# The last step of a block inverse: the inverse added by VectorE at the eviction instead of by identity products on TensorE

## The reference, cut to what matters

```python
S = S * exp(g_t)
mem = einsum('bhk,bhkv->bhv', k_t, S)
delta = (v_t - mem) * b_t
S = S + einsum('bhk,bhv->bhkv', k_t, delta)
o_t = einsum('bhk,bhkv->bhv', q_t * scale, S)
```

## Time and profile before

| | before |
|---|---|
| median of 3 executions | 4767.14 us (4764.29 to 4769.24) |
| span of the profiled execution | 4761.7 us |
| TensorE matmul busy | 4665.0 us (98%) |
| VectorE busy | 4138.2 us (87%) |
| ScalarE busy | 3397.1 us (71%) |
| GpSimd busy | 3152.1 us (66%) |

### The profile page before, as it was taken

How to read it: one execution, slowest core, us unless ns; L and a number is a source line. 1 busy time by engine, 2 the same in 40 slices (tenths; PEclk the granted TensorE clock), 3 DMA queues, 4 the chain that set the end, 5 groups by cost and what they waited for, 6 DMA issues and landing times. The chain is left out here.

```text
span 4761.7 us, 140986 instructions
## 1 busy us (share of the span) xinstructions
PE 4665.0 (98%) x44336; PEld 3733.8 (78%) x44336; DVE 4138.2 (87%) x9914; ACT 3397.1 (71%) x10287; POOL 3152.1 (66%) x4511
## 2 busy tenths in 40 slices
PE   6999999999999999999999999999999999999798
PEld 4788888888888888888888888888888888888566
DVE  6888888888888888888888888888888889999576
ACT  5777777777777777777777777777777777777443
POOL 5666666666666666666666666666666666777565
PEclk9999999999999999999999999999999999999899
DMA  5111111111111111111111111111111111121000
GB/s 180 48 33 44 33 53 34 44 37 47 46 34 44 33 53 33 44 33 51 36 44 35 42 50 36 44 34 50 35 44 33 44 42 53 47 61 44 29 29 34
DMA packets 206732, 212.94 MB, mean 45 GB/s; under 512 B 17218, under 2 KB 180180, under 8 KB 206036
## 3 DMA queue, kind: packets, MB, share of 16 engines
q1 hardware_dynamic: 206036, 204.06, 14.0%
HBM read 186.31 MB, written 17.70 MB: 43 GB/s over the span
## 5 line engine op out<-in xcount | busy, mean ns | idle before, releaser
L1074 DVE SCALAR_TENSOR_TENSOR cv<-ps_a,wqkv,cv 128x511 f32<-128x511 f32 (+2 forms) x1536 | 1145.8, 746 | 181.6 <-ACT cv L1067 161.0
L1279 POOL TENSOR_TENSOR bm<-bat,mask 128x256 f16<-128x256 f32 x1536 | 1029.5, 691 | 0.6
L1059 PE MATMUL ps_a<-xin,wqkv 128*128 128x512 f32 x2048 | 1002.8, 612 | 3.0 <-DVE bat L1256 1.5
L1329 ACT ACTIVATE m<-b 128x256 f16<-128x256 f32 x1536 | 597.2, 389 | 376.2 <-PE b L1324 376.2
L1067 ACT ACTIVATE cv<-ps_a,wqkv 128x512 f32<-128x512 f32 x512 | 352.0, 688 | 554.3 <-PE ps_a L1059 554.1
L1340 DVE TENSOR_TENSOR tt<-tt,b 128x256 f16<-128x256 f16 x1536 | 635.4, 414 | 115.4 <-PE b L1335 114.8
L1382 ACT CAST tt<-bu 128x256 f16<-128x256 f32 x1536 | 578.2, 376 | 1.2 <-PE bu L1377 0.5
L1514 PE MATMUL ps_a<-wout,yT 128*128 128x256 f32 x2048 | 548.3, 390 | 0.5 <-ACT yT L1508 0.5
L1059 PEld LDWEIGHTS ps_a<-xin,wqkv 128*128 128x128 f32 x2048 | 349.6, 191 | 250.6 <-issue 250.6
L1207 PE MATMUL ps_b<-wgate,xin 128*128 128x256 f32 x2048 | 494.9, 384 | 0.2 <-DVE vtok L1230 0.2
L1256 DVE SCALAR_TENSOR_TENSOR bat<-ps_a,w,dec 128x256 f32<-128x256 f32 x1024 | 435.4, 477 | 40.5 <-DVE w L1126 22.4
(11 more groups left out here) (270 smaller groups left out, 12229.8 us busy)
## 6 DMA issues: line engine op xcount, KB each, us to landing
xin<-xT_scratch SPq DMA_DIRECT2D x128, 512.0 KB, 4.0
grow<-g_scratch SPq DMA_DIRECT2D x256, 256.0 KB, 4.6
gam<-g_scratch SPq DMA_DIRECT2D x256, 96.0 KB, 2.8
n_x<-in_x SPq DMA_DIRECT2D x16, 512.0 KB, 4.9
xT_scratch<-acc SPq DMA_DIRECT2D x16, 512.0 KB, 5.9
out_y<-e_yo SPq DMA_DIRECT2D x16, 512.0 KB, 2.6
gate_tok<-in_x SPq DMA_DIRECT2D x56, 128.0 KB, 2.9
wqkv<-in_w_qkv SPq DMA_DIRECT2D x32, 128.0 KB, 3.1
```

The source lines that it names most:

```text
L1059: ins = pe.matmul(ps[:], wqkv[:, k, j * P:(j + 1) * P], xin[p][:, k, :], start=k == 0, stop=k == KT - 1)
L1074: s.done(dve.scalar_tensor_tensor(y[:, r:], ps[:, 0:T - r], tap[:, j, TAPS - 1 - r:TAPS - r], y[:, r:], ALU.mult, ALU.add), f"a_tap{j}{r}")
L1279: s.done(pool.tensor_tensor(half_of(bm[:, l, units(g), :], l, 1), half_of(bt[:, units(g), :], l, 1), half_of(c["mask"][:, l, :].unsqueeze( ...
L1329: s.done(act.mul(half_of(m1[:, l, units(g), :], l, 0), half_bank(bank, l), -1.0), f"b_Me{l}{g}")
```

## The change

`b_F{g}` loses the four products with the identity. `b_T{g}` moves from ScalarE to VectorE and becomes an addition of the bank and `tt[:, 1]`. `b_t2{g}` of the next item, on GpSimd, now waits for `b_T{g}` instead of `b_F{g}`, because `tt[:, 1]` is read by it. In the written order two entries are placed anew: `b_T0.2` stands ahead of `a_tap22.1`, and `b_T1.2` behind `c_R1.2`; the order of all other steps stays.

```diff
-    c_yT2.3 x_y0.5 x_y1.5 b_diag0.1 b_vT0.2 b_t20.1 c_acc1.3 a_tap22.1 c_R3.3 y_sh.0 b_Me31.2 b_T0.2 a_tap23.1
+    c_yT2.3 x_y0.5 x_y1.5 b_diag0.1 b_vT0.2 b_t20.1 c_acc1.3 b_T0.2 a_tap22.1 c_R3.3 y_sh.0 b_Me31.2 a_tap23.1
...
-    c_KS1.2 c_acc3.3 c_p0.2 b_vT1.1 b_E0 b_V20.1 a_tap02 b_U20.1 b_F1.2 b_T1.2 c_R1.2 a_proj1 k_turn.0 c_Z1.2 b_t21.1
+    c_KS1.2 c_acc3.3 c_p0.2 b_vT1.1 b_E0 b_V20.1 a_tap02 b_U20.1 b_F1.2 c_R1.2 b_T1.2 a_proj1 k_turn.0 c_Z1.2 b_t21.1
...
                 if (yield f"b_t2{g}"):
                     s.need(pool, i, f"b_diag{g}")
-                    s.need(pool, i - 1, f"b_F{g}")
+                    s.need(pool, i - 1, f"b_T{g}")
...
                     for k in range(4):
                         u = 4 * g + k
-                        pe.matmul(bank[:, k * P:(k + 1) * P], r16[:, u, :], tt[:, 1, u, :], start=True, stop=False)
-                        ins = pe.matmul(bank[:, k * P:(k + 1) * P], tt[:, 0, u, :], c["ident16"][:], start=False,
-                                        stop=True)
+                        ins = pe.matmul(bank[:, k * P:(k + 1) * P], r16[:, u, :], tt[:, 1, u, :], start=True, stop=True)
                     s.done(ins, f"b_F{g}")
                 if (yield f"b_T{g}"):
-                    s.need(act, i, f"b_F{g}")
-                    s.need(act, i - 2, f"c_Z{2 * g + 1}")
-                    s.done(act.copy(tinv[p][:, units(g), :], in_units(bank)), f"b_T{g}")
+                    s.need(dve, i, f"b_F{g}")
+                    s.need(dve, i - 2, f"c_Z{2 * g + 1}")
+                    s.done(dve.tensor_tensor(tinv[p][:, units(g), :], in_units(bank), tt[:, 1, units(g), :], ALU.add),
+                           f"b_T{g}")
```

## The result

The changed kernel takes 4792.08 us (median of 4 runs, 4791.67 to 4799.81) beside 4765.72 us for the kernel before in the same session (4763.52 to 4769.24, 4 runs): a ratio of 1.0057, 95% interval 1.0046 to 1.0069. It is 26 us slower; the forecast was 20 us slower, in a range that holds 4792.

What follows compares the result with a forecast made beforehand. TensorE was taken as never without work in the attention, with VectorE's chain to the gate close behind. 125 slots x (0.14 - 0.01) = 16 us plus 4 us for late slots, over 4767.1, gave 4787 us, range 4760 to 4812 us.

Steps and rivals of the forecast that it cites:

- The bound: In the attention: TensorE is never without work, but the next chain, on VectorE, may be close behind.
- The removal: In b_F: dropping the identity products frees 0.45 us of TensorE a slot; ScalarE's relief counts as nothing.
- The addition: New b_T on VectorE, once a group: costs 0.60 us to the next start, bounds 0.41 and 0.68 us.
- The gate: Product b_g waits for b_vtok: at least 2.57 us from b_vtok's start to the step behind the gate.
- The sum: Whole kernel: 125 slots give 16 us, late slots 4 us, so 20 us over 4767.1, 4787 us.
- The two groups: In each slot: slack 0.61 us in group 0, 0.46 us in group 1; changes of -0.01 and +0.14 us.
- The late slots: 14 slots with residual steps: c_R2 delays c_Z2, about 0.3 us a slot more, 4 us in all.
- Does the delay end there?: Behind the gates: VectorE's idle times of 0.51 and 0.31 us and smaller waits absorb the delay; nothing further in ordinary slots.
- Rival 3: Behind the gates VectorE does not catch up: 47 us more, 4834 us; chance 0.09.
- GpSimd: b_t2 now waits for b_T: b_t20 follows 0.64 us later, and b_Tq0 does not wait for it.
- Rival 1: TensorE keeps what it was relieved of: slots shorten by 0.45 us, 4709 us; chance 0.12.
- Rival 2: Both sizes nearly cancel, chains 0.05 to 0.1 us shorter: within 0.2%, about 4767 us; chance 0.17.

Runs made afterwards that it cites:

- e1: Kernel before without its identity products; b_T stays a copy on ScalarE, no addition: 4717.23 us, ratio 0.9896.
- e2: Changed kernel with the four identity products put back into b_F, so VectorE's addition is all that is new: 4834.42 us, ratio 1.0141.
- e7: Change made in group 0 alone; group 1 keeps identity products, ScalarE's copy and the old place of b_T1: 4768.17 us, ratio 0.9999.
- e3: Changed kernel with a second, needless addition of half the size behind each b_T on VectorE: 4879.34 us, ratio 1.0236.
- e4: Changed kernel with the addition over two of a group's four units only: 4730.35 us, ratio 0.9919.
- e10: Changed kernel reordered: b_vtok ahead of a conv tap in both groups, a_tanh2 behind c_u3, a_silu2 behind a_tap33, b_hi1 behind b_Ue20: 4788.85 us, ratio 1.0043.
- e12: As e10, but b_Ve31 ahead of b_vtok0 and a_tap23 on VectorE, and b_Ve30 ahead of the statistics: 4743.37 us, ratio 0.9949.
- e8: Changed kernel reordered: b_vtok ahead of a conv tap, a_tanh2 and a_silu2 later, b_hi0 and b_hi1 behind b_Me00 and b_Me01: 5467.99 us, ratio 1.147.

## Why the prediction was right

**The bound.** TensorE dense, but VectorE close behind at one point: borne out. With the products gone alone TensorE stays dense at 33.22 us a slot (e1).

**The removal.** Predicted 0.45 us a slot, measured 0.45 (33.67 to 33.22, e1). That ScalarE's relief gives nothing was not run by itself; in e2, where the copy is gone too, the groups come within 0.07 us of the sum without it.

**The addition.** Predicted 0.60 us to the next start; in the changed kernel it is 2021.69 - 2021.09 = 0.60 us, with 687 ns recorded for the group. The Trainium skill's figure (VectorE: DVE Perf Modes, the TRN2 errata) gave 0.66 us; that lies near the recorded duration and above the distance to the next start, and the queue moves by the latter. With it the forecast would have been 4802 us, 10 us too high instead of 5 too low.

**The gate.** Predicted 2.57 us from the start of `b_vtok` to the step behind the gate; measured 2.57 us in group 0 (2009.91 - 2007.34) and 2.56 us in group 1 (2025.76 - 2023.20). A price read from one early row of the filling pipeline held in the steady state. One remark on it was too general: that a gate which waited takes 0.10 us longer holds for group 1 alone. In group 0 the gate that did not wait took 1.81 us already (2027.84 - 2026.03), and there the restart costs 0.02 us. The sum is not touched, since it goes by the 2.57 us.

**The two groups.** Predicted -0.01 and +0.14 us, measured 0.00 and +0.14 us, and e7 shows the zero of group 0 by itself. The sum over the slots was right to 1 us.

**The late slots.** Predicted 14 slots with 0.3 us on top of what the ordinary ones lose, measured twelve with 0.36 us on top (0.50 less 0.14): 4 us either way. The waits of TensorE's weight loads in one of them:

```profile
4088.99 1.59 PEld L1207 LDWEIGHTS ps_b<-wgate,xin 128*128 128x128 f32 x8 [0.34 <-DVE vtok L1230]
4093.85 0.30 PEld L1402 LDWEIGHTS cs<-state,kqs 128*128 128x128 f32 x2 [0.19 <-DVE state L1463]
4095.44 0.52 PEld L1419 LDWEIGHTS cs<-rr,tinv 128*128 128x128 f32 x4 [0.30 <-DVE rr L1407]
```

The predicted wait for `c_R2` is there; the one for the state's update is one more, since VectorE has no idle time ahead of it here.

**What the sum lacked** is a term of 4 us: the thirty slots that are 0.14 us longer than the rest, which make most of the difference between the 20 us forecast and the 26 us of the slots. In 24 of them it is `c_O3` (line 1448) that starts 0.25 to 0.28 us behind its forerunner and not 0.12 to 0.14 us. It waits for six semaphores, and the rows of ScalarE and VectorE around it stand at the same distances in a slot that has it and in one that hasn't. What it waits for is open. The runs narrow it: it comes in e2, e3 and e7 too, and with 0.20 to 0.22 us in e4, which all have the addition in group 0, and hardly ever in e10 and e12 (once in some 220 slots), where `a_tanh2` stands behind `c_u3`. The sum also has nothing for the 5.1 us ahead of the first `b_F0` and the 2.3 us less behind the slots; that they partly cancel, and the medians differ by 26 us like the slots, is luck. The prediction had compared slots of the kernel before, found one length, and taken one length for granted after.

**Does the delay end there?** Yes, but barely. The 0.51 us of VectorE's idle time ahead of the state's update has shrunk to 0.17 us:

```profile
2027.79 0.48 DVE L1463 SCALAR_TENSOR_TENSOR state<-state,gend,cs 128x256 f32<-128x256 f32 x1 [0.17 <-issue]
```

Rival 3 fell (TensorE waits for no other step in every slot), and e3 shows that even 0.33 us more a group arrives one for one and does not add up over the slots.

**GpSimd.** `b_t20` is 0.65 us later and nothing is held by it. The 82 us of waits put down to GpSimd's masks in e10 were not GpSimd's, as e12 showed.

**The rivals.** Rival 1, all kept, is what e1 and e4 look like (4717 and 4730 us): it needed an addition under 0.24 us in group 1, and with 0.33 us the slots were indeed 0.10 us above the floor. Rival 2, nearly cancelling, is what group 0 does. The Trainium skill's rule (Perfetto Trace Analysis, Identifying the Most-Contended Engine) to relieve first the engine with the highest occupancy was read too quickly in the prediction. TensorE has 98% by its matmuls, but the page sets that figure aside and takes for TensorE, among others, the busy share of its weight loads, which is 78% here and below VectorE's 87%. Read so, the rule does not say that the change is a gain, and the loss does not speak against it. Nor does it give the size or the place of the loss: e4 and e12 also put work on VectorE and were faster. The slack of the next chain decided.

## What to carry to other kernels

When work moves off an engine that is busy all the time, write down the slack of the chain that receives it, place by place. The time moves by the larger of what the first chain gives back and what the second exceeds its slack by, group by group, and one busy share of 98% beside one of 87% says nothing of that. If the change loses, look at what stands behind the new step in the queue before giving it up: here another order of some ten steps turned 26 us of loss into 27 us of gain, after three orders that did not. And when an order is changed, follow each moved step on the queues of the engines that wait for it; an engine that runs ahead of the list stalls on a step that looks early enough, and in e8 TensorE's idle time was followed by products at the lower clock, which cost 280 us more.

## What the runs showed of the hardware

- A release costs time of its own, and not always the same: `b_Ve31` ended at 2003.83 by its row, the weight load that waited for it came at 2003.95 (e10), 0.12 us later; the load of the gate comes 0.05 us behind the recorded end of `b_vtok` in each of its 186 named waits.
- A gate product of eight matmuls that had to wait takes 1.83 us instead of 1.73 us in group 1 (2025.76 - 2023.93, against 2009.88 - 2008.15 before), but in group 0 1.83 us instead of 1.81 us (2009.91 - 2008.08, against 2027.84 - 2026.03 before). What a wait at the head of a series costs beyond itself depends on what stands ahead.
- TensorE's granted clock stayed at 1.00 through the gate waits of up to 0.4 us each (changed kernel, 174 to 4000 us) and fell to 0.50, the 1.2 GHz level, with the idle time of 2.48 us in e8.
- Wait names can change where nothing has changed in time: loads of line 1420 stood at 120.5 us in 504 waits for "issue" before; after, the same loads stand at 90.4 us in 378 waits for "issue" and 35.9 us in 141 waits for `rr`. Nearly all of those 141 are the usual 0.24 us between two loads under another name.
